# Linear attention: running sums on four 64x64 quadrants of the PE array, and key sums once per group

## What is computed

```python
q = feature_map(ln(x) @ wq + bq); k = feature_map(ln(x) @ wk + bk); v = ln(x) @ wv + bv   # 16 heads of 8
S = S + einsum('bhd,bhe->bhde', kt, vt)        # running over the 64 rows of a sequence
z = z + kt
num = einsum('bhd,bhde->bhe', qt, S)
den = einsum('bhd,bhd->bh', qt, z)[..., None] + EPS
out_t = num / den                              # then x = x + out @ wo + bo
```

## Time and profile before

| | us |
|---|---|
| median of 3 runs (lowest, highest) | 632.59 (632.16, 632.62) |
| profiled execution, first to last instruction | 631.7 |
| median less that span | 0.9 |
| the attention's steady slots, by the 16 `on` instructions | 40.3 to 256.3, 14 slots |

### The profile page before, as it was taken

The page is one execution under the profiler, slowest core; times in us unless marked ns, Lnnn a source line. Parts: engine busy times, 40 slices in busy tenths (PEclk is TensorE's granted clock), DMA queues, the critical chain, the costliest instruction groups (busy, mean ns, idle before and its releaser), DMA issues.

```text
span 631.7 us, 15833 instructions
## 1 busy us (share of the span) xinstructions
PE 575.6 (91%) x3838; PEld 442.8 (70%) x3839; DVE 517.9 (82%) x1602; ACT 420.2 (67%) x1188; POOL 427.0 (68%) x461
## 2 busy tenths in 40 slices
PE   3899999999999999968799877999999999999993
PEld 1455555555555555545689644799999999989993
DVE  5599999999999999983678888566877887877883
ACT  3557777877787777351788512345788888878882
POOL 2899989998999899310877600765467666757762
PEclk9999999999999999999999968899999999999998
DMA  5610111111161111283477551221012111111110
GB/s 147 184 51 0 35 33 35 34 33 33 33 100 33 34 33 34 66 119 90 119 208 202 113 113 29 53 51 46 27 49 54 48 47 47 51 38 51 51 44 23
DMA packets 49973, 40.92 MB, mean 65 GB/s; under 512 B 21971, under 2 KB 40278, under 8 KB 49926
## 3 DMA queue, kind: packets, MB, share of 16 engines
q1 hardware_dynamic: 44150, 29.61, 19.0%
q0 software_dynamic: 4960, 10.49, 6.4%
q10 hardware_dynamic: 816, 0.26, 0.2%
HBM read 27.47 MB, written 12.88 MB: 64 GB/s over the span
## 4 chain that ended last, share of the span: by engine, by line
PE 63%; ACT 12%; DVE 12%; issue 6%; DMA 4%; POOL 1%; DVEq 0%; ACTq 0%; SPq 0%; POOLq 0%
PE bank L1329 57%; PE bank L1333 4%; ACT xh L671 3%; ACT xs L773 2%; PE bank L1568 2%; DMA w_s<-gram_d 1%; DVE on L935 1%; ACT ex L647 1%; ACT nb_c L668 1%; DVE mean_early L1037 1%; DMA circ<-prob_d 1%; PE bank L1492 1%; ACT rl L648 1%; ACT xrT L759 1%; ACT ex L653 1%
## 5 line engine op out<-in xcount | busy, mean ns | idle before, releaser
L542 POOL TENSOR_TENSOR shared<-v,qk 128x1152 f32<-128x1152 f32 x64 | 142.8, 2231 | 2.8
L1329 PE MATMUL bank<-shared,tri_s 128*128 128x360 f32 (+1 forms) x384 | 137.2, 494 | 0.7 <-DVE R L896 0.7
L609 POOL DMA_INDIRECT shared<-xs_d,row_u x91 | 87.8, 964 | 62.2 <-DVE row_u L1227 31.6
L896 DVE TENSOR_TENSOR R<-bank,qk 128x360 f32<-128x360 f32 (+1 forms) x192 | 96.2, 540 | 8.6 <-PE bank L1329 6.7
L1329 PEld LDWEIGHTS bank<-shared,tri_s 128*128 128x128 f32 x384 | 69.8, 192 | 44.9 <-issue 20.4
L616 POOL DMA_INDIRECT out_x<-shared x64 | 63.6, 993 | 48.4 <-DVE shared L1299 21.8
L905 DVE TENSOR_REDUCE nd<-R 128x144 f32<-128x1152 f32 x64 | 86.1, 1346 | 1.6
L1329 PE MATMUL bank<-w_s,hid 128*128 (+1 forms) x620 | 82.3, 276 | 0.1
L1329 PEld LDWEIGHTS bank<-w_s,hid 128*128 128x128 f32 x620 | 75.5, 192 | 0.6 <-issue 0.3
L812 ACT ACTIVATE shared<-bank 128x256 f32<-128x256 f32 x155 | 59.4, 384 | 21.9 <-PE bank L1329 16.2
L1320 DVE TENSOR_TENSOR hid<-bank,shared 128x256 f32<-128x256 f32 x155 | 61.4, 422 | 10.0 <-ACT shared L812 9.8
(11 more groups left out here) (247 smaller groups left out, 1138.4 us busy)
## 6 DMA issues: line engine op xcount, KB each, us to landing
xs_d<-xs SPq DMA_DIRECT2D x16, 270.0 KB, 4.7
X<-in_x SPq DMA_DIRECT2D x16, 256.0 KB, 2.8
ct<-in_ctx_t SPq DMA_DIRECT2D x16, 256.0 KB, 2.8
ct<-in_ctx_r SPq DMA_DIRECT2D x16, 256.0 KB, 3.6
gram_d<-gd SPq DMA_DIRECT2D x14, 256.0 KB, 2.4
w_s<-in_w_experts SPq DMA_DIRECT2D x8, 384.0 KB, 4.0
circ<-prob_d SPq DMA_DIRECT2D x30, 64.0 KB, 2.7
shared<-xs_d,row_u POOLq DMA_INDIRECT x91, 2.6
```

Source lines behind the costliest of these rows:

```text
L542: nc.gpsimd.tensor_tensor(outer[k], v9[k % 2][:].unsqueeze(3).broadcast_to([P, H, D1, D]), kk.unsqueeze(2).broadcast_to([P, H, D1, D]), AL ...
L609: nc.gpsimd.indirect_dma_start(xg[q], None, xs_d[:, :], bass.IndirectOffsetOnAxis(ap=rows, axis=0)).then_inc(xg_in[q], 16)
L896: nc.vector.tensor_tensor(R[:, lo:hi], bank[2 + c][:, 0:n_h * D1 * D].rearrange("p (h e d) -> p h e d", h=n_h, e=D1), qq.unsqueeze(2).broa ...
L1329: return nc.tensor.matmul(o, l, r, start=start, stop=stop, skip_group_check=True)
```

## The change

The ones of `v9` go, so `outer[k]` has 1,024 columns and holds S alone. `tri_s` is zero between the two sequences, so the product is made of blocks: for each sequence b and each half c of the heads one product of a 64x64 block, with 512 columns, into partitions c*64.. of a PSUM area `run` of two banks. The partitions of `run` are then (half of the heads, row in the sequence), the columns (sequence, head, e, d). To meet it, q and k of that layout are needed: `project` writes k and v as before (256 columns), and q by four products of 64x64 columns. The sum z is taken per group: `key_sums`, four products with 256 columns, the stationary operand being 64 columns of `tri_s`, into bank 4; `key_dots` multiplies them with q (512 columns, tile `zq`), `sum_dots` sums over d into `den`. `times_q` is one product over 1,024 columns, `sum_heads` sums 1,024 columns to 128. `turn_quotients` brings `on` back with 16 products of 64x64x64 in place of four transposes. The reciprocal moves from the next slot to the end of the same slot, and `quotients` from after the first piece of tile 1 to after `times_q` of tile 0. Semaphores and the sizes of buffers follow.

```diff
+            def turn_quotients():
+                settle(pe)
+                for k in range(GT):
+                    for b in range(2):
+                        for c in range(2):
+                            own = slice(c * HALF, c * HALF + HALF)
+                            last = mm(bank[5][own, k * P + b * HALF:k * P + b * HALF + HALF],
+                                      on[own, k, b * HALF:b * HALF + HALF], id_s[own, own])
+                return last
             def running_sums(g, p, r, k):
                 t = GT * g + k
                 pe.wait_ge(a_outer, t + 1)
-                for c, (lo, hi) in enumerate(HEADS):
-                    need(pe, b_mul, 3 * (t - 1) + c + 1)
-                    mm(bank[2 + c][:, 0:(hi - lo) * D1 * D], tri_s[:], outer[k][:, lo:hi].rearrange("p h e d -> p (h e d)")
-                       ).then_inc(b_run, 1)
+                need(pe, b_mul, t)
+                settle(pe)
+                for b in range(2):
+                    for c in range(2):
+                        own = slice(b * L, b * L + L)
+                        last = mm(run[c * L:c * L + L, b * 512:b * 512 + 512], tri_s[own, own], outer[k][own, c * 512:c * 512 + 512])
+                last.then_inc(b_run, 1)
+            def key_sums(g, p, r):
+                pe.wait_ge(a_f, GT * g + GT)
+                need(pe, b_dots, 2 * g - 1)
+                for b in range(2):
+                    for c in range(2):
+                        last = mm(bank[4][c * L:c * L + L, b * GT * HALF:(b + 1) * GT * HALF], tri_s[:, b * L:b * L + L],
+                                  qk[p][:, :, E + c * HALF:E + c * HALF + HALF])
+                last.then_inc(b_keys, 1)
             def project(g, p, r, k):
...
-                mm(bank[1][:, 0:3 * E], xT[:, k * P:(k + 1) * P], wqkv[:]).then_inc(a_proj, 1)
+                mm(bank[1][:, E:3 * E], xT[:, k * P:(k + 1) * P], wqkv[:, E:3 * E])
+                for b in range(2):
+                    for c in range(2):
+                        last = mm(bank[1][c * L:c * L + L, b * HALF:b * HALF + HALF], xT[:, k * P + b * L:k * P + b * L + L],
+                                  wqkv[:, c * HALF:c * HALF + HALF])
+                last.then_inc(a_proj, 1)
...
 +            def key_dots(g, p, r):
+                dve.wait_ge(b_keys, g + 1)
+                nc.vector.tensor_tensor(
+                    zq[:].rearrange("p (k b x) -> p b k x", k=GT, b=2), bank[4][:].rearrange("p (b k x) -> p b k x", b=2, k=GT),
+                    qk[p][:, :, 0:E].rearrange("p k (b x) -> p b k x", b=2), ALU.mult).then_inc(b_dots, 1)
+            def sum_dots(g, p, r):
+                dve.wait_ge(b_dots, 2 * g + 1)
+                need(dve, c_rden, g)
+                nc.vector.tensor_reduce(den[:], zq[:].rearrange("p (x d) -> p x d", d=D), AX.X, ALU.add).then_inc(b_dots, 1)
```

More of the change, by code:

```diff
@@ L16 @@
 D = E // H
-D1 = D + 1
 T = B * L
@@ L129, in build @@
         ex, rl = [sb(f"ex{i}", [P, 2 * E]) for i in range(2)], [sb(f"rl{i}", [P, 2 * E]) for i in range(2)]
-        v9 = [sb(f"v9_{i}", [P, H, D1]) for i in range(2)]
+        v8 = [sb(f"v8_{i}", [P, E]) for i in range(2)]
         qk = [sb(f"qk{i}", [P, GT, 2 * E]) for i in range(2)]
-        shared = sb("shared", [P, GT * H * D1 * D])
+        shared = sb("shared", [P, 9 * GT * E])
         bias_f, bias_r, bias_a, bias_b = (shared[0:3, i * NBIAS:(i + 1) * NBIAS] for i in range(4))
         b_wide = shared[:, 4 * NBIAS:4 * NBIAS + 3 * E]
-        outer = [shared[:, i * H * D1 * D:(i + 1) * H * D1 * D].rearrange("p (h e d) -> p h e d", h=H, e=D1)
-                 for i in range(GT)]
-        R = sb("R", [P, H, D1, D])
-        nd = [sb(f"nd{i}", [P, GT, H, D1]) for i in range(2)]
+        outer = [shared[:, i * D * E:(i + 1) * D * E] for i in range(GT)]
+        R = sb("R", [P, (D + 1) * E])
+        num = [sb(f"num{i}", [P, GT, E]) for i in range(2)]
+        zq = sb("zq", [P, GT * E])
         den, rden = sb("den", [P, GT * H]), sb("rden", [P, GT * H])
@@ L236, in build, with psum @@
         y0 = sb("y0", [P, E])
-        bank = [ctx.enter_context(nc.psum_tensor(f"bank{i}", [P, 512], F32)) for i in range(8)]
+        def psum(name, banks=1):
+            return ctx.enter_context(nc.psum_tensor(name, [P, banks * 512], F32))
+        bank = [psum("bank0"), psum("bank1")]
+        run = psum("run", 2)
+        bank += [run[:, i * 512:(i + 1) * 512] for i in range(2)] + [psum(f"bank{i}") for i in range(4, 8)]
         settled = sem("settled")
@@ L505, in _ @@
             pool.memset(power[:], -0.5).then_inc(setup, 1)
-            for k in range(2):
-                pool.memset(v9[k][:], 1.0).then_inc(setup, 1)
             pool.memset(ones_f[:], 1.0).then_inc(setup, 1)
@@ L531, in features @@
                 pool.wait_ge(a_ex, t + 1)
-                need(pool, b_mul, 3 * (t - 2 * GT) + 3)
+                need(pool, b_mul, t - 2 * GT + 1)
+                need(pool, b_dots, 2 * (g - 1) - 1)
                 need(pool, a_outer, t - 2 * GT + 1)
@@ L539, in outer_product @@
                 pool.wait_ge(a_pev, 3 * t + 3)
-                need(pool, b_run, 3 * (t - GT) + 3)
+                need(pool, b_run, t - GT + 1)
                 kk = qk[p][:, k, E:2 * E].rearrange("p (h d) -> p h d", h=H)
+                vv = v8[k % 2][:].rearrange("p (h e) -> p h e", h=H)
                 nc.gpsimd.tensor_tensor(
-                    outer[k], v9[k % 2][:].unsqueeze(3).broadcast_to([P, H, D1, D]),
-                    kk.unsqueeze(2).broadcast_to([P, H, D1, D]), ALU.mult).then_inc(a_outer, 1)
+                    outer[k].rearrange("p (h e d) -> p h e d", h=H, e=D), vv.unsqueeze(3).broadcast_to([P, H, D, D]),
+                    kk.unsqueeze(2).broadcast_to([P, H, D, D]), ALU.mult).then_inc(a_outer, 1)
             def slot(n, i):
@@ L655, in denominators @@
             def denominators(g, p, r):
-                act.wait_ge(b_red, GT * g + GT)
-                need(act, c_rden, g)
-                nc.scalar.activation(den[:], nd[p][:, :, :, D].rearrange("p t h -> p (t h)"), ACT.Copy, bias=ATT_EPS).then_inc(c_den, 1)
+                act.wait_ge(b_dots, 2 * g + 2)
+                nc.scalar.activation(den[:], den[:], ACT.Copy, bias=ATT_EPS).then_inc(c_den, 1)
             def negative_mean(g, p, mv, mv_sem, mr, mr_sem):
@@ L674, in slot @@
             def slot(n, i):
-                a0, a1, c, d = (stage(n, i, s) for s in (2, 1, -1, -2))
+                a0, a1, b, c, d = (stage(n, i, s) for s in (2, 1, 0, -1, -2))
                 if i is None and n == 1:
@@ L958, in slot @@
                 if b:
-                    times_q(*b, 1, (1, 2))
+                    sum_heads(*b, 0)
+                    key_dots(*b)
+                    times_q(*b, 1)
                 if a0:
@@ L1372, in slot @@
                 if b:
+                    key_sums(*b)
                     running_sums(*b, 1)
@@ L1391, in slot @@
                     pe.wait_ge(c_on, c[0] + 1)
-                    transposes(bank[5], on).then_inc(c_tr, 1)
+                    turn_quotients().then_inc(c_tr, 1)
                 if i is None and n == NG:
```

69 lines of the change are left out of this document (32 added, 37 removed).

## The result

| | before | after |
|---|---|---|
| median of 4 runs (lowest, highest), us | 632.54 (632.16, 632.62) | 672.67 (671.16, 672.95) |
| ratio (95% interval) | 1 | 1.0623 (1.0606 to 1.0640) |
| first to last instruction of the profiled execution, us | 631.7 | 671.2 |
| first to fifteenth `on`, us | 40.3 to 256.3 | 37.1 to 293.35 |

What follows compares the result with a forecast made beforehand. PE, DVE and POOL all stood close to the bound; a new ring of waits would lengthen fourteen slots from 15.43 to 16.0 or 16.5 us. With -1.7 at the ends, 638.9 or 645.9; forecast the middle, 642 us, range 630 to 656.

Steps and rivals of the forecast that it cites:

- The sign: Whole kernel: the change makes it slower, given a chance of 0.78.
- the new wait: PE's key sums wait over 1 us for POOL's fourth features, closing a ring of 16.0 us per slot, against 15.43.
- the work per slot: Attention slot: by work alone PE, DVE and POOL each lose 0.7 to 0.8 us.
- ahead of and behind the 14 slots: Ends of the attention: -1.0 us from five POOL outer products ahead, -0.7 from DVE in the last slot, together -1.7.
- eight steps of 0.058 us and a tail of 0.17: PE's 64-column records run in pairs; at 0.058 per step, turning the quotients takes 0.93 us against 0.44.
- The sum of the ring: Slot: POOL's stretch 9.7, start 0.1, PE 0.86 + 0.15 + 0.86, handover 0.25, DVE 4.06; 16.0 us.
- The rival in which quadrants run in pairs: PE: running sums cost 1.72 us per tile, PE's slot 17.5 us, time 660 us; pairs or worse given 0.10.
- `mv_a` to the fourth features' end: POOL's stretch from DVE's moments to the last features, 10.37 less three outer-product savings of 0.21: 9.7 us.
- All the rest of that ring: From the fourth features' end through PE's key sums and running sums 1 and DVE's products to the end of `mv_a`.
- the ring over `mv_a`: Loop of waits through POOL, PE and DVE's moments sets the slot, 16.0 to 16.5 us; as forecast given 0.70.
- 1.19 was the forecast: `on` starting ahead of POOL's fourth features slows them from 0.73 to 1.19 us, lengthening the ring to 16.5.
- clearly below DVE's: PE's busy time falls below DVE's: about 14 us of work per slot against some 14.5.

Runs made afterwards that it cites:

- moments_early: Changed kernel with DVE's statistics `st_a` moved ahead of the product with the key sums and moments `mv_a` ahead of product 1; 672.39 us, 1.0634.
- warm: Changed kernel plus six filler products of ones, results unread, in PE's idle time ahead of the key sums; 663.65 us, 1.0485.
- keys_third: Changed kernel with key sums behind running sums 3, the turn between `project` 0 and 1, `ct` behind the `wo` product, DVE and ACT parts moved accordingly; 629.71 us, 0.9957.
- before_wait: Kernel before, with only one wait added: PE waits for all four tiles' features ahead of running sums 1; 659.86 us, 1.0414.
- project_full: Changed kernel with each `project` again one product of 384 columns, q in the old layout; 664.22 us, 1.0517.

## Why the prediction was wrong, step by step

**What held.** The sign; the place of the new wait (PE ahead of the key sums, 1.7 to 1.8 us for POOL's `qk`, "over 1 us"); the work per slot. The sizes of the pieces, those of PE from one start to the next in the slot of 148.54:

| | predicted, us | measured, us |
|---|---|---|
| running sums of one tile, and a change of form | 0.86 + 0.15 | 1.02 |
| key sums, and a change of form | 0.86 + 0.15 | 1.01 |
| `project`, two changes of form | 0.66 + 0.30 | 1.01 |
| POOL's outer product | 1.97 | 1.96 |
| DVE's product with q | 1.21 | 1.22 |
| sum of `zq` | 0.68 | 0.68 |
| PE's work in a slot | about 14 | 14.2 |
| DVE's work in a slot | some 14.5 | 14.5 |
| ahead of and behind the 14 slots | -1.7 | -0.8 |

One step of its working does not add up: eight steps of 0.058 us and a tail of 0.17 are 0.63, not the 0.69 of the earlier trace rows. With 0.065 the turn would have been 1.04 us instead of 0.93; it took 0.98 and its tail. The sum of the ring does not use it.

The rival in which quadrants run in pairs did not come true: eight records of 512 columns in 1.09 us are four at a time (2 x 0.43 and the tail), as the Trainium skill (TensorEngine Tiling (Array Packing), Overview, "The Solution") has it. Its 660 us lie nearer to the result than my 642, but by its own mechanism it would show running sums of 1.7 us, and there are none at full clock.

**What failed: "The new wait", the term "`mv_a` to the fourth features' end".** I put it at 9.7 us, read as 10.37 less three savings from a stretch in which POOL had no gap. It measured 11.4 (the end of `mv_a`, 154.71, to 166.09). All the rest of that ring, from the end of the fourth features ahead of the key sums (148.41) to that of `mv_a`, measured 6.30 against 6.28. The difference is waits that were not there before, 0.62 us for ACT's exponential of tile 2, 0.60 ahead of the fourth features (the exponential of tile 3 ends at 164.83, 0.35 behind the outer product) and 0.17 ahead of `ve_c`, and 0.29 by which these features ran slower beside `on`. I had asked what POOL waits for, but had taken its inputs from ACT to be in time, since they were so in a trace in which PE hardly stood. The change does not touch the order of ACT's evacuations, and ACT was 67% busy; it is nowhere in the sum. But ACT takes its list strictly in order, and at the top of that list stand two things that come from PE behind the key sums. A delay of PE is a delay of ACT's whole stretch of 10 us, and at the end of that stretch is what PE waits for.

So the ring was the wrong one, and not just too short: less POOL's 1.2 us of waits for ACT's exponential, the measured slot leaves 16.5 for the ring over `mv_a`, within the 16.0 to 16.5 of the forecast. `moments_early` shows it: `mv_a` came over 4 us earlier and the time did not change. The longest term of the right sum stood in the trace of before, where ACT's list already ran from `oT` to the exponential of tile 3 in 9.8 us without a gap over 0.17:

```profile
134.46 0.60 ACT L693 ACTIVATE oT<-bank 128x512 f32<-128x512 f32 x1 [1.14 <-PE bank L1333]
...
143.87 0.41 ACT L653 ACTIVATE ex<-ex 128x256 f32<-128x256 f32 x1
```

The others are 1.4 us from that exponential to the key sums and PE's pieces up to the turn (1.01 + 1.01 + 1.01 + 1.08 + 1.01 + 1.2). With all pieces as measured in the changed kernel the slot is 17.7 us, and 632.6 + 14 x (17.7 - 15.43) - 0.8 = 663.6 us at full clock; `warm` measured 663.65. That is a sum made afterwards, so its closeness checks the account and is no forecast.

**What the prediction did not ask: the clock.** The prediction took every PE duration at the clock of before, 1.00 in all stretches of the earlier trace rows. It named a wait of over 1 us per slot on PE and had no term for what PE's clock does then. By `warm` this is worth 9 us. Of the 30.7 us between the forecast and the result, some 22 are the wrong ring and 9 the clock.

**What came about, and cost less than the ring:** `on` began 0.24 us ahead of the fourth features, these took 1.02 us instead of 0.73 (1.19 was the forecast), and `on` stayed at 0.68.

**PE below DVE.** I had expected PE's busy time to fall "clearly below DVE's". Between 60 and 250 us it is 154.6 against 151.6. In the slot at full clock it is a little below (14.2, 14.5); the stretches at half clock add to PE's.

**Why `keys_third` gains no more.** The fourteen slots of its profile (38.1 to 247.96 us, 14.99 each) gain 6.2 us on those of before, and the first `on` comes 2.2 earlier. The slot behind them takes 4.2 back: 16.13 us from the fifteenth `on` to the sixteenth, against 11.92. There `on` began together with an outer product and took 2.50 us, PE's turn waited for it, and the clock was at half from 249.3 to 256.1:

```profile
247.96 1.96 POOL L547 TENSOR_TENSOR shared<-v,qk 128x1024 f32<-128x1024 f32 x1
247.96 2.50 DVE L949 TENSOR_TENSOR on<-num,rden 128x512 f32<-128x512 f32 x1
```

With 0.9 less behind that slot the sum is 5.1 us, the difference of the two spans (631.7 and 626.6). The profiled run was the shortest of the twelve; of the others there are no slots to read, and their mean granted clock was lower (0.971 to 0.982 against 0.988).

**Left open.** Why the clock falls in some of these slots and not in others, with the same pause ahead. The length of the pause alone does not decide it: in `before_wait` PE stood for 1.6 to 2.0 us ahead of the same place in every slot, and its clock stayed at 1.00 from 43 to 330 us.

## What to carry to other kernels

When a change adds a wait to an engine, walk the ring from that wait over every engine whose list is fed from behind it, also those whose code the change does not touch, and add up each list from what arrives late to what is waited for: an engine that is 60% busy has no slack if its work comes as one stretch behind an input. Then move the waiting instruction to where its input is old and nobody waits for its engine; here moves in the engines' order alone took the changed kernel from 672.7 to 629.7 us. And where a change adds a pause to PE on every turn, ask for the clock too: here it cost 9 us in one kernel, and in another with pauses as long it did not fall.

## What the runs showed of the hardware

- Behind pauses of 1.7 us on PE the granted clock went to half in every third slot of the attention's middle, and 1.09 us of running sums then took 1.99; behind the same pause in the other slots, and behind pauses of 1.6 to 2.0 us in `before_wait`, it stayed at 1.00. Six filler products in the pause kept the clock at 1.00 from 25 to 397 us, and took 9 us off.
- Four 64x64 quadrants run fully side by side in fp32 (1.09 us for eight records of 512 columns, which need 1.72 in pairs), and 64-column records in two quadrants run in pairs, though they write to one PSUM bank: the turn's 32 records took 1.15 us from the first start to the last end (153.67 to 154.82), where one after the other they need 32 x 0.054 = 1.7 by the price of the earlier trace rows.
- A change of the array's form costs some 0.15 us, an estimate: running sums of a tile take 1.02 us from start to start where their columns need 0.86. It does not hide: a projection in two forms took 1.01 us to the start of the next piece, one plain product of 384 columns 0.75 to 0.84 (`project_full`).
- DVE's product `on` and POOL's large products hold each other up in both directions, and which one waits depends on who is first by a tenth of a microsecond. In the kernel before, an `on` that began 0.01 us ahead of an outer product (194.40) took 0.68 us and the outer product 2.71; one that began 0.14 behind (147.40) took 2.59 beside 2.18. `on` took 1.9 to 2.0 in nearly every slot of `before_wait`, and 2.50 once in `keys_third`, where it began with an outer product.
